# A fused whitening, Fourier filter and MLP kernel: the first MLP matmul in plain fp32 on two 64-row parts of the array, and the second one slice later

## The reference

```python
x = whiten(x)                                   # inv_sqrt @ (x - mean), gamma, beta
residual = x
h = layer_norm(x, n1_g, n1_b)
xf = rfft2(h, axes=(1, 2))                      # 8 blocks of 8 channels
o1 = relu(complex xf @ w1 + b1)
o2 = softshrink(complex o1 @ w2 + b2, 0.01)     # v - sign(v)*lam where abs(v) > lam, else 0
h = irfft2(o2) + h                              # afno_filter adds its own input
h = h + residual
residual = h
h = layer_norm(h, n2_g, n2_b)
h = gelu(h @ mw1 + mb1)                         # 64 -> 256
out = h @ mw2 + mb2 + residual                  # 256 -> 64
```

## Time and profile before

| | |
|---|---|
| time, median of 3 runs | 1033.61 us (1033.3 to 1036.7) |
| profiled execution | 1037.1 us, its span 1035.2 us |
| busy share of the span | PE 88%, PEld 75%, DVE 69%, ACT 54%, POOL 25% |
| one step of the loop | 103.3 us, e.g. 466.78 to 570.04 |
| its slices | 497.36 to 567.02 |
| last MLP alone | from 973.64 to the end |

### The profile page before, as it was taken

One profiled execution on the slowest core, in us unless ns is written; L12 is line 12 of the kernel. 1 busy time (PEld: TensorE's weight loads), 2 busy tenths in 40 slices (PEclk: granted clock), 3 DMA queues, 4 the chain that ended last, 5 costly groups with the idle time before them and its releaser, 6 DMA issues.

```text
span 1035.2 us, 18451 instructions
## 1 busy us (share of the span) xinstructions
PE 908.7 (88%) x6263; PEld 775.4 (75%) x6263; DVE 716.5 (69%) x2061; ACT 557.1 (54%) x1139; POOL 261.0 (25%) x107
## 2 busy tenths in 40 slices
PE   5888973887999988998899889988998999799687
PEld 5886552765689768976897689768976997499465
DVE  4356779169957876877677777877788688543762
ACT  0002001674777586757675767586748754875333
POOL 2000001333332234223422342234315324330110
PEclk8995556889999999999999999999999999899789
DMA  9950202002000020002000200110000000000001
GB/s 258 233 125 1 62 1 62 2 1 62 2 10 28 28 63 9 27 19 71 9 27 22 68 11 25 33 57 18 18 27 1 20 27 20 0 28 26 11 28 36
DMA packets 9956, 40.78 MB, mean 39 GB/s; under 512 B 1232, under 2 KB 1232, under 8 KB 8208
## 3 DMA queue, kind: packets, MB, share of 16 engines
q1 hardware_dynamic: 9888, 40.00, 14.3%
HBM read 27.15 MB, written 12.85 MB: 39 GB/s over the span
## 4 chain that ended last, share of the span: by engine, by line
PE 53%; DVE 21%; issue 10%; ACT 9%; DMA 6%; DVEq 0%; SPq 0%; ACTq 0%
PE psum L1045 16%; PE psum L1030 8%; PE psum L983 8%; DMA n<-x_dram 6%; ACT p_y L1133 5%; PE psum L964 4%; DVE stats L539 4%; PE psum L930 3%; ACT o_g L1142 3%; PE psum L918 3%; PE psum L1004 3%; PE psum L857 3%; DVE o_g L294 2%; PE psum L905 2%; PE psum L1016 2%
## 5 line engine op out<-in xcount | busy, mean ns | idle before, releaser
L1174 ACT ACTIVATE hid<-psum,hbias 128x448 f32<-128x448 f32 x224 | 136.1, 633 | 141.4 <-PE psum L1030 140.5
L1045 PEld LDWEIGHTS psum<-prm,hid 128*112 128x112 f32 x1792 | 186.2, 182 | 8.5 <-ACT hid L1174 4.5
L1045 PE MATMUL psum<-prm,hid 128*112 128x96 f32 x1792 | 190.5, 266 | 2.2 <-ACT hid L1174 2.2
L364 POOL TENSOR_TENSOR hbuf<-hbuf,prm 112x1792 f32<-112x1792 f32 x15 | 51.6, 3439 | 337.5 <-DVE hbuf L613 337.5
L662 DVE TENSOR_TENSOR n2T<-psum,n2T 64x448 fp32r<-64x448 f32 x112 | 69.7, 622 | 94.4 <-ACT n2T L1166 93.1
L1030 PE MATMUL psum<-n2T,mw1h 128*128 128x448 f32 x224 | 103.3, 461 | 30.0 <-DVE n2T L662 17.4
L392 POOL TENSOR_TENSOR p_y<-over,under 116x512 f32<-116x512 f32 x64 | 77.5, 1212 | 167.1 <-ACT under L1192 167.0
L983 PE MATMUL psum<-cst,p_y 116*128 116x224 f32 (+1 forms) x480 | 101.8, 355 | 3.0 <-POOL p_y L392 3.0
L983 PEld LDWEIGHTS psum<-cst,p_y 116*128 116x128 f32 (+1 forms) x480 | 89.9, 194 | 6.2 <-POOL p_y L392 3.2
L1133 ACT COPY p_y<-psum 64x232 f32<-64x232 f32 (+1 forms) x256 | 84.3, 329 | 13.9 <-PE psum L940 10.3
L1030 PE MATMUL psum<-n2T,mw1l 128*128 128x448 f32 x224 | 84.1, 376 | 0.0
(11 more groups left out here) (114 smaller groups left out, 1714.2 us busy)
## 6 DMA issues: line engine op xcount, KB each, us to landing
xin<-x_dram SPq DMA_DIRECT2D x9, 1568.0 KB, 8.6
out_dram<-oslice SPq DMA_DIRECT2D x56, 224.0 KB, 2.2
ybuf<-x_dram SPq DMA_DIRECT2D x2, 1568.0 KB, 21.5
fbuf<-x_dram SPq DMA_DIRECT2D x2, 1568.0 KB, 25.1
n<-x_dram SPq DMA_DIRECT2D x2, 1568.0 KB, 28.5
xin<-x_dram SPq DMA_DIRECT2D x4, 392.0 KB, 6.0
prm<-params_dram SPq DMA_DIRECT2D x1, 771.5 KB, 29.7
cst<-consts_dram SPq DMA_DIRECT2D x1, 652.0 KB, 21.1
```

The source lines that it names most:

```text
L1045: last = nc.tensor.matmul(t[0:ROWS, at:at + 96], hid[:, m, w % 2, (w // 2) * ROWS:(w // 2 + 1) * ROWS], pp("mw2")[:, 128 * m + zeros:128 * ...
L1174: nc.scalar.activation(hid[:, q % 2, q // 2, :], ring_c[k % RING_C][:, 0:4 * ROWS], ACT.Gelu, bias=hbias[:, q % 2:q % 2 + 1]).then_inc(c_a ...
```

## The change

Five things change together.

1. The first MLP matmul. n2T is one plain copy of the bank, 128x448 (ACT, one instruction for four). Its partitions 0 to 63 hold one token of a column pair and 64 to 127 the other. mlp_in does, for one half m of the hidden units, two plain fp32 matmuls: v = 0 reads partitions 0 to 63 of weight and data, v = 1 partitions 64 to 127, into banks 0 and 1 of ring_c. There is no mw1h, no mw1l and no remainder on DVE.
2. The order. A slice is now mlp_in(s, 0), fill(0), the second matmul of the slice before (mlp_out(s - 1)), fill(1), mlp_in(s, 1), fill(2), transposes for s + 1, fill(3). hid is double. The last mlp_out of a pair stands before inv_h(4) on PE; on DVE its ev_mlp stands between ev_inv_h 5 and 6.
3. The banks. ring_b has three, ring_c three: hidden units in 0 and 1, transposes and outputs in 2.
4. The shrinkage. DVE clamps the value to -0.01 and 0.01 (clamped) behind the addition of the bias, and POOL subtracts that from the value; the two Relu are gone.
5. The mean of the second LayerNorm is folded into the weights: n2 is fbuf times 1/std (one DVE operation a half instead of two), and a matmul in setup takes the weights' column mean out of mw1s.

```diff
-A_CHUNKS, C_CHUNKS = 14, 42
-RING_A, RING_B, RING_C = 2, 4, 2
-C_ACT, C_DVE = 28, 14
+A_CHUNKS = 14
+RING_A, RING_B, RING_C = 2, 3, 3
...
+B_BANK = [k % RING_B for k in range(B_CHUNKS)]
+B_BEFORE = before_in_bank(B_BANK)
+
+
+C_ORDER = [("n2", 0)]
+for _s in range(SLICES):
+    C_ORDER += [("hid", _s, 0, 0), ("hid", _s, 0, 1)]
+    if _s > 0:
+        C_ORDER.append(("out", _s - 1))
+    C_ORDER += [("hid", _s, 1, 0), ("hid", _s, 1, 1)]
+    if _s < SLICES - 1:
+        C_ORDER.append(("n2", _s + 1))
+C_ORDER.append(("out", SLICES - 1))
...
+C_BANK = [what[3] if what[0] == "hid" else 2 for what in C_ORDER]
...
-                        a, b = (m[:, c % L2_BUFS, 0:n].rearrange("p (k m j) -> p k m j", m=4, j=CH) for m in (over, under))
+                        a, b = (m[:, c % L2_BUFS, 0:n].rearrange("p (k m j) -> p k m j", m=4, j=CH) for m in (layer2, clamped))
                         nc.gpsimd.tensor_tensor(yk, a, b, ALU.subtract).then_inc(y_ready, 1)
...
+                    link(nc.vector.scalar_tensor_tensor(mw1s[:], mwm_ps, -float(ROWS) / C, mw1s[:], ALU.mult, ALU.add))
...
+                def multiply_rstd(i, k):
+
+                    nc.vector.tensor_tensor(half_w(n2, k), half_w(fbuf, k), bc(small[:, 8, k * WP:(k + 1) * WP], WP),
+                                            ALU.mult).then_inc(n2_ready, 1)
...
-                            dve.wait_ge(shrunk, i * 8 + c - L2_BUFS + 1)
+                            dve.wait_ge(y_ready, i * 8 + c - L2_BUFS + 1)
...
+                        nc.vector.tensor_scalar(clamped[:, c % L2_BUFS, 0:n], layer2[:, c % L2_BUFS, 0:n], LAM, -LAM,
+                                                ALU.min, ALU.max).then_inc(shrunk, 1)
...
+                def mlp_in(i, s, m):
+
+                    if m == 0:
+                        pe.wait_ge(c_act, i * C_ACT + C_ACT_DONE["n2", s])
+                    for v in range(2):
+                        t = free_c(i, C_AT["hid", s, m, v])
+                        nc.tensor.matmul(t[:, 0:4 * ROWS], mw1s[C * v:C * v + C, HH * m:HH * m + HH],
+                                         n2T[C * v:C * v + C, :], start=True, stop=True).then_inc(pe_c, 1)
...
                 def mlp(i, s, fill):
 
...
+                    mlp_in(i, s, 0)
+                    fill(0)
+                    if s > 0:
+                        mlp_out(i, s - 1)
+                    fill(1)
+                    mlp_in(i, s, 1)
                     fill(2)
                     if s < SLICES - 1:
                         transpose_n(i, s + 1)
                     fill(3)
...
-                    for v in range(2):
-                        nc.scalar.copy(n2T[C * v:C * v + C, v, :],
-                                       ring_c[k % RING_C][C * v:C * v + C, 0:4 * ROWS]).then_inc(hi_ready, 1)
...
+                    nc.scalar.copy(n2T[:], ring_c[C_BANK[k]][:, 0:4 * ROWS]).then_inc(c_act, 1)
```

More of the change, by code:

```diff
@@ L95, with before_in_bank @@
 X_BESIDE = {1: [[0], [], [1], []], 2: [[2], [], [3], []], 3: [[4], [5], [6], []]}
-def lo_done(s):
-    return 1 if s == 0 else 2 * s
-def out_done(s):
[L105 to L117, removed]
+def before_in_bank(banks):
+    last = {b: k for k, b in enumerate(banks)}
+    out = []
+    for k, b in enumerate(banks):
+        out.append((last[b], k <= last[b] and b not in banks[:k]))
+        last[b] = k
+    return out
+B_BANK = [k % RING_B for k in range(B_CHUNKS)]
[9 more added lines that the diff above has]
+C_ORDER.append(("out", SLICES - 1))
+C_CHUNKS = len(C_ORDER)
+C_AT = {what: k for k, what in enumerate(C_ORDER)}
+C_BANK = [what[3] if what[0] == "hid" else 2 for what in C_ORDER]
+C_BEFORE = before_in_bank(C_BANK)
+C_ACT_DONE = {what: n + 1 for n, what in enumerate(what for what in C_ORDER if what[0] != "out")}
+C_ACT, C_DVE = len(C_ACT_DONE), SLICES
+def out_done(s):
+    return s + 1
 CONST_COLS = {"f1": 2 * KR, "f2": 4 * KF, "invw": 2 * 224, "invh": ROWS, "mask1": 128, "mask2": 128,
@@ L709, in step, with slice_ @@
                 def step(i, ahead, behind):
[L710 to L717 removed]
+                    def slice_(s, e0, e1, e2, e3):
+                        e0()
+                        if behind and s > 0:
+                            ev_mlp(i - 1, s - 1)
+                        e1()
+                        e2()
+                        e3()
                     def next_(what, *args):
@@ L844, in covariance @@
                     last.then_inc(s_pe, 1)
+                    nc.tensor.matmul(mwm_ps, pilot_w[0:C, :], mw1s[0:C, :], start=True, stop=True).then_inc(s_pe, 1)
                 def factor():
@@ L1089, in step @@
                     slice_(6, lambda j: (turn(i, [4 + j]), inv_h(i, j)))
-                    for k in range(4, 8):
-                        inv_h(i, k)
+                    if behind:
+                        mlp_out(i - 1, SLICES - 1)
+                    inv_h(i, 4)
+                    inv_h(i, 5)
+                    inv_h(i, 6)
+                    inv_h(i, 7)
                 covariance()
@@ L1197, in slice_ @@
                         if behind:
-                            gelu(i - 1, s, fill)
+                            mlp(i - 1, s, fill)
                         else:
```

272 lines of the change are left out of this document (109 added, 163 removed).

## The result

The kernel after takes 1057.3 us (median of 4 runs, 1056.5 to 1060.1), the kernel before beside it 1033.5 (4 runs, 1031.6 to 1036.7): ratio 1.026, 95% interval 1.0227 to 1.0294. It is slower, as forecast, but by 24 us and not by 69. The profiled execution's span is 1055.7 us against 1035.2, so 20.5 us are to be found in the traces.

A forecast was written before the change was run, and what follows sets the result against it. PE was taken to bound the slices. First matmul +68.9, shared excursion -3.0, n2T hop +10.5, head -0.7 and last pair -7 sum to +68.7 us, giving 1102 us, range 1035 to 1148.

The forecast's parts named there:

- Streams: First MLP matmul in each slice: the pair overlaps partly, 1.125 us a pair, 2.25 a slice against 1.88, +0.37.
- wholly side by side: Rival on the first MLP matmul: the pair takes 0.75 us, 42 us less than forecast, 1060 us; chance 14%.
- Excursions: First MLP matmul: going to 64 rows and back costs 0.43 us, two a slice, +0.86 us (bounds 0 and 0.86).
- the excursion that slice 5 shares: Once a step the pair of slice 5 follows the 58-row L983 directly, saving 7 x 0.43, -3.0 us.
- The n2T hop: PE's waits for the n2T copy, 3.0 us a step, less 1.5 us of waits that go: net +10.5 us.
- old waits: PE's waits at the first MLP matmul in slices 1 to 6, 1.5 us a step, which go.
- The head: Start of each step, up to the first MLP matmul: 33.5 us against 33.6, -0.7 us over seven steps.
- the stall at the first DFT: At the start of a step PE idles about 1.6 us before the first DFT, naming DVE's fbuf.
- The last pair: Final MLP, where nothing fills: waits go, -11, copy behind two gelus, +7.5; with other terms -7 us (bounds -15, +2).
- The clamps: Eight a step on DVE, at most 0.7 us each: nothing; 2 to 5 us if DVE set slice 2 or 3.
- Setup: Before the loop, one matmul against two DVE operations: nothing.

The follow-up runs named there:

- the kernels with 64 and with 128 rows: Kernel after with both matmuls of a pair on rows 0 to 63: 1130.8 us; with all 128 rows and zero weights on the other half: 1093.4 us.

## Why the prediction missed, and what of it held

The forecast was +69 us and +24 were measured. The direction and the reason hold: PE bounds the slices, relieving DVE and ACT buys little, and the plain fp32 pair costs PE more than eight fp32r matmuls. By its own steps:

- **Streams: the step that failed.** "The second record of A needs A's rows again and must wait for its first, B's first can then run beside A's second, and B's second follows: three lengths a pair, 1.125 us." The trace shows B's first record starting 7 ns behind A's first, and B's second behind A's second: two lengths of stream, 0.75 us, which the kernel with both on the same rows confirms with +0.75 a pair. I read program order as the order of starts: each matmul is one instruction to the program, and its two records follow each other on its own rows, not in one row with those of its neighbour. Streams therefore save 0.38 us a slice against the earlier trace rows (1.50 against 1.88) instead of adding 0.37. Over 56 slices the step is wrong by 42 us; with 0.75 in its place the same sum gives 1060 us, against 1057.3 measured. That is the rival "wholly side by side", to which I gave 14%. The Trainium skill ("TensorE: Matmul & The Clock Gate", Part 3) gives some 4 ns between starts on different row groups; this trace has 7 in most pairs, and 0.11 us in those behind a wait.
- **Excursions: right.** 0.43 forecast, 0.42 around the pair, 0.39 between the kernels with 64 and with 128 rows, 0.32 around a single short matmul. With two a slice, the first matmul is 2 x (0.75 + 0.42) = 2.34 us a slice, +0.46 against 1.88 and +26 in all, where I had +1.23 and +68.9. The Trainium skill ("TensorEngine Tiling", Key Properties) says that a change of the tiling mode drains the array; the kernels with 64 and with 128 rows agree with it. The 3.0 us for the excursion that slice 5 shares were not measured by themselves.
- **The n2T hop: right in place, near in size.** 2.2 us a step against 3.0, in four waits: 0.70 behind slice 0 (I had 0.8), 0.18 behind 1 and 2 (0.4 each), 1.19 behind 5 (1.2). There is none behind 3 (0), and behind 4 (0.2) only the raw records show one, of 0.12. The 1.5 us of old waits are gone. Net +0.7 a step, not +1.5: over 5 us less than I had. What I didn't have is the 0.11 by which B is late behind such a wait, some 0.5 us a step.
- **The head: right.** 32.84 us against 33.60, -0.8 a step (I had -0.1): the stall at the first DFT is 1.22, not 1.6, and names DVE's fbuf as said. What I costed as part of a small gain is, by the runs with the fold and with three banks alone, two large terms that cancel: the fold's 14 us and the bank's 11 to 14.
- **The last pair: the mechanism right.** -3.9, of which the pairs of seven slices are 7 x 0.46 = +3.2, so waits and LN2 gave -7.1; I had -7. A slice takes 6.96 us (1015.35 to 1022.31) against 7.03, with a wait for the copy of 1.13 where I had 1.25. A wait of 3.81 us of the last inv_h for DVE's fbuf, ahead of the last MLP, I didn't have; n2 is no longer waited for there (5.97 before).
- **The clamps: right,** nothing (1.0003). **Setup:** I had nothing; it is -2.7, within the scatter of setups.

## What to carry to other kernels

Two matmuls on different rows of the array are worth their overlap only if both can start at once: operands there and both banks free, since here a bank that came 0.9 us late turned 0.95 us into 1.90 without any idle time in the view of the matmuls. Price a switch to fewer rows by its frame as well as by its stream; here two excursions a slice (0.84 us) ate more than the 0.38 that the streams saved. When several edits come as one, build each alone first: here the one that paid (the fold, -14 us) was bundled with a form that needed a bank (+11) and cost PE 26.

## What the runs showed that I had not expected

- Two plain fp32 matmuls of two records each, on rows 0 to 63 and 64 to 127, start 7 ns apart in both records; four records of 448 columns take 0.95 us, of which 0.20 belong to the excursion, and 1.70 on the same rows. If B starts late, the pair is longer by as much.
- The excursion isn't one figure: 0.42 us around a pair of 448 columns, 0.32 around a single matmul of 64.
- The six steps of pairs 1 to 6 in the kernel before have a granted clock of 0.98 in two (104.3 and 103.3 us, 362.48 to 570.04) and 1.00 in the others (102.3 and 101.9 behind them). In the kernel after all six have 1.00, and the first five last 105.85 to 105.95. So about 1 us of the step that I took my rows from was clock, and at full clock the step grew by 3.5 to 4 us, not by 2.6. The windows of the kernel before show the place (columns as above, the granted clock third from the end):

```profile
492.87:494.87 2.00, 2.00 (x16) 1.80 (x16) 1.95 (x4) 1.94 (x4) 2.00 (x1) 1.00 0.00 0
497.36:498.36 1.00, 1.00 (x3) 0.85 (x4) 1.00 (x2) 0.00 (x0) 1.00 (x1) 0.50 0.00 0
498.36:500.00 1.64, 1.64 (x10) 1.64 (x9) 0.19 (x1) 0.63 (x1) 1.64 (x1) 0.50 0.00 0
```

Behind PE's idle of 2.49 us (494.87 to 497.36) the clock is at the lower of its two levels, 1.2 GHz, for 2.6 us and more. The same idle of 2.49 in the step that starts at 570.04 leaves it at 1.00: in 601 to 603 it is still full. So the wait costs its own length in each step and a further 1 us in some, and I had costed the first part alone.
